# Summing the mixer's coefficients once per four pairs, and a closing product in two passes

## The reference, cut to what matters

```python
xn = layernorm(x)
x = x + gnn(xn) + mix(xn)                 # gnn: attention, 16 heads of 64, mask from 12288 edges
x = x + ffn(layernorm(x))
# mix, per head of 64 columns:
q, k = exp(-square(xn @ Wq + bq) / 2), exp(-square(xn @ Wk + bk) / 2)
coeff = sum(q * k, axis=head columns)     # one number per row and head
mix = (coeff * (xn @ Wv + bv)) @ Wo + bo
# ffn: one of 8 experts is picked (argmin of a loss over the data), then
h = relu(x @ Wd + bd)                     # 64 wide
ffn = (x @ base_W.T + base_b) + (h @ Wu + bu) @ Wc.T + bc
```

## Time and profile before

| What | us |
|---|---|
| median of three runs (476.05, 479.64, 480.69) | 479.64 |
| the profiled execution, its own time | 474.66 |
| its span, first to last instruction | 472.9 |
| PE busy | 465.9 |
| DVE busy | 342.3 |
| ACT busy | 262.2 |
| POOL busy | 157.2 |

### The profile page before, as it was taken

One profiled execution on the slowest core, in us unless ns is written; L12 is line 12 of the kernel. 1 busy time (PEld: TensorE's weight loads), 2 busy tenths in 40 slices (PEclk: granted clock), 3 DMA queues, 4 the chain that ended last, 5 costly groups with the idle time before them and its releaser, 6 DMA issues.

```text
span 472.9 us, 7361 instructions
## 1 busy us (share of the span) xinstructions
PE 465.9 (99%) x2533; PEld 432.4 (91%) x2533; DVE 342.3 (72%) x796; ACT 262.2 (55%) x429; POOL 157.2 (33%) x176
## 2 busy tenths in 40 slices
PE   7999999999999999999999999999999999999996
PEld 5999999999999888999999999999998888888885
DVE  6979966677626259687978888796966794587294
ACT  3734433333324245788989889897974542163170
POOL 3147677777767741002130202212142000050200
PEclk9999999999999999999999999999999999999999
DMA  8877756655444454577675766766679835210463
GB/s 243 325 230 230 239 195 167 176 182 180 154 152 153 133 200 179 175 226 253 205 232 184 235 192 197 247 180 224 192 240 382 308 115 179 89 46 0 155 247 133
DMA packets 39049, 91.92 MB, mean 194 GB/s; under 512 B 7410, under 2 KB 20306, under 8 KB 38884
## 3 DMA queue, kind: packets, MB, share of 16 engines
q1 hardware_dynamic: 33604, 83.15, 54.0%
q0 software_dynamic: 4832, 7.45, 4.7%
q10 hardware_dynamic: 576, 0.85, 0.5%
HBM read 77.96 MB, written 13.47 MB: 193 GB/s over the span
## 4 chain that ended last, share of the span: by engine, by line
PE 87%; DVE 5%; DMA 3%; ACT 3%; issue 1%; SPq 0%; DVEq 0%; ACTq 0%
PE PS L1278 32%; PE PS L1288 28%; PE PS L1283 16%; PE PS L1416 3%; PE PS L1404 2%; DMA turn<-U 2%; PE PS L1535 2%; PE PS L1346 2%; DMA U<-x 1%; DVE U L1076 1%; DVE w_lo L895 1%; PE PS L1266 1%; ACT U L659 1%; PE PS L1539 1%; ACT w_hi L536 1%
## 5 line engine op out<-in xcount | busy, mean ns | idle before, releaser
L895 DVE TENSOR_TENSOR w_lo<-raw,w_hi 128x1024 fp32r<-128x1024 f32 x86 | 104.4, 1225 | 45.0 <-ACT w_hi L536 45.0
L536 ACT ACTIVATE w_hi<-raw 128x1024 fp32r<-128x1024 f32 x87 | 90.8, 1054 | 68.5 <-PE PS L1288 44.1
L454 POOL DMA_INDIRECT table<-evalue,where x96 | 103.0, 1073 | 45.7 <-issue 25.2
L1283 PE MATMUL PS<-xT_hi,w_lo 128*128 128x384 f32 x320 | 61.9, 334 | 0.0
L1278 PE MATMUL PS<-xT_hi,w_hi 128*128 128x384 f32 x320 | 61.9, 334 | 0.0
L1278 PE MATMUL PS<-xT_lo,w_hi 128*128 128x384 f32 x320 | 61.9, 334 | 0.0
L1278 PEld LDWEIGHTS PS<-xT_lo,w_hi 128*128 128x128 f32 x320 | 56.0, 188 | 0.0
L1278 PEld LDWEIGHTS PS<-xT_hi,w_hi 128*128 128x128 f32 x320 | 56.0, 188 | 0.0
L1283 PEld LDWEIGHTS PS<-xT_hi,w_lo 128*128 128x128 f32 x320 | 56.0, 188 | 0.0
L469 POOL TENSOR_TENSOR T_lo<-U,T_hi 128x384 fp32r<-128x384 f32 x8 | 8.2, 1020 | 97.8 <-ACT T_hi L733 97.8
L1288 PE MATMUL PS<-w_hi,T_hi 128*128 128x512 f32 x144 | 40.0, 391 | 0.0
(11 more groups left out here) (241 smaller groups left out, 817.1 us busy)
## 6 DMA issues: line engine op xcount, KB each, us to landing
raw<-weights SPq DMA_DIRECT2D x84, 512.0 KB, 4.6
turn<-U SPq DMA_DIRECT2D x16, 576.0 KB, 4.0
U<-turn SPq DMA_DIRECT2D x64, 144.0 KB, 2.9
U<-key_dram SPq DMA_DIRECT2D x32, 192.0 KB, 4.1
mask<-weights SPq DMA_DIRECT2D x9, 512.0 KB, 5.1
...
```

The source lines that it names most:

```text
L454: pool.indirect_dma_start(tables[g], bass.IndirectOffsetOnAxis(ap=where[:, k:k + 1], axis=0), evalue[:, k:k + 1], None, bounds_check=N * N ...
L536: act.activation(w_hi[slot][:], raw[slot][:], ACT.Copy).then_inc(hi_ready[slot], 1)
L895: dve.tensor_tensor(w_lo[slot][:], raw[slot][:], w_hi[slot][:].bitcast(F32), ALU.subtract).then_inc(lo_ready[slot], 1)
L1283: last = pe.matmul(o, wl, src[0][:, k, :], start=False, stop=(k == KB - 1))
```

## The change

Four edits.

- **Coefficients.** The mixer's columns are permuted on the host so that a group of four pairs (`GROUP`) holds 16 columns (`SHARE`) of each of its eight heads in every pair. The four tiles of exponentials are added up (`feat_sum`), split once, and one pair of matmuls gives the coefficients of all four. The raw values wait in `raw_value(j)`, slices of the attention values that are no longer read, and DVE multiplies four of them after pairs 3 and 7. `mix_hi` and `mix_lo` run four pairs later.
- **x ahead.** POOL issues the fetch of x after `mix_lo(4)`, ahead of the last three, and the fetch of the bias rows after `mix_lo(5)`.
- **Base weights.** The four spare base blocks are loaded and split two blocks later.
- **Close.** Rows 64 to 127 of the P tile hold P again, and `h_main` holds the high part of h over its low part, so one matmul does two passes; `h_side` by `pc[1]` does the third and the side rows (the biases in parts, one row that `h_main` gives up to a row of ones). Row 64's work goes through one row written by ACT. Tile (0, 1) is copied by ACT and added by POOL, DVE adds the other five.

```diff
+def adds(j):
+    return j - j // GROUP
...
@@ -388,19 +414,17 @@
                 load_weights(*slot_use(n + 3), weights[35 + n])
             for b in range(5, 16):
                 load_weights(*C_USES[b], weights[72 + b])
-                if b == 5:
-                    sp.wait_ge(vs_ready, KB)
                 if b == 7:
+                    sp.wait_ge(ml_ready, KB)
                     sp.wait_ge(score_read, KB * 6 + 1)
-                if 5 <= b < 9:
-                    load_weights(*E_USES[(b - 5)], weights[72 + 16 + (b - 5)])
+                if 7 <= b < 11:
+                    load_weights(*E_USES[(b - 7)], weights[72 + 16 + (b - 7)])
             for e in range(4, 8):
                 load_weights(*E_USES[e], weights[72 + 16 + e])
             sp.wait_ge(x2_turned, NT)
...
-            for half in range(2):
+            for half, t, done, count in ((0, 0, y_ready, 1), (0, 2, y_ready, 2), (1, 0, y_ready, 3),
+                                         (0, 1, y_added, 1), (1, 1, y_ready, 4), (1, 2, y_ready, 5)):
                 c = slice(half * HALF, (half + 1) * HALF)
-                for t in range(NT):
-                    sp.wait_ge(y_ready, half * NT + t + 1)
-                    sp.dma_start(out[t * P:(t + 1) * P, c], x_rows[:, t, c]).then_inc(stored, 16)
+                sp.wait_ge(done, count)
...
@@ -488,43 +514,48 @@
                                    ALU.subtract).then_inc(vs_ready, 1)
             for j in range(KB):
-                if j:
+                if j >= GROUP:
                     pool.wait_ge(vs_ready, j)
-                    mix_lo(j - 1)
-                    pool.wait_ge(ml_ready, j)
+                    mix_lo(j - GROUP)
+                    pool.wait_ge(ml_ready, j - GROUP + 1)
                 values(j)
                 if j:
                     pool.wait_ge(vs_ready, j + 1)
                     out_lo(j - 1)
                     pool.wait_ge(ol_ready, j)
-                if j == KB - 1:
+            for j in range(KB - GROUP, KB):
+                mix_lo(j)
+                pool.wait_ge(ml_ready, j + 1)
+                if j == KB - GROUP:
+                    pool.wait_ge(pT_ready, KB * 2 - 1)
+                    pool.wait_ge(block_ready, KB * 6)
+                    pool.wait_ge(feat_ready, KB // GROUP)
+                    pool.dma_start(x_rows, x.rearrange("(t p) d -> p t d", p=P)).then_inc(xr_in, 16)
+                if j == KB - GROUP + 1:
                     pool.wait_ge(ql_ready, KB)
                     pool.dma_start(row_bo, rows[0:2, :].partition_broadcast(P)).then_inc(rows_in, 16)
-            mix_lo(KB - 1)
-            pool.wait_ge(ml_ready, KB)
-            pool.wait_ge(pT_ready, KB * 2 - 1)
-            pool.wait_ge(block_ready, KB * 6)
-            pool.wait_ge(feat_ready, KB)
-            pool.dma_start(x_rows, x.rearrange("(t p) d -> p t d", p=P)).then_inc(xr_in, 16)
             out_lo(KB - 1)
             pool.wait_ge(ol_ready, KB)
...
-            pool.memset(t0l[:, 0:2 * D].bitcast(F32), 0.0).then_inc(aug_zero, 1)
...
+            pool.memset(h_side[R:P, :].bitcast(F32), 0.0).then_inc(side_const, 1)
+            pool.wait_ge(side_const, 1)
+            pool.memset(h_side[R:R + 1, :].bitcast(F32), 1.0).then_inc(side_const, 1)
+            pool.wait_ge(side_const, 2)
+            pool.memset(h_side[side, :].bitcast(F32), 1.0).then_inc(side_const, 1)
+            pool.wait_ge(side_const, 3)
+            pool.memset(pc[1][SIDE_ROW:P, :].bitcast(F32), 0.0).then_inc(pc_zero, 1)
+            pool.wait_ge(pc_zero, 1)
             split_lo(*E_USES[7])
+            pool.wait_ge(hT_hi, 1)
+            pool.tensor_copy(h_side[0:R, :], h_main[0:R, :].bitcast(F32)).then_inc(h_copied, 1)
+            pool.wait_ge(h_low_in, 2)
+            pool.memset(h_main[R:R + 1, :].bitcast(F32), 1.0).then_inc(hT_ready, 1)
+            pool.wait_ge(y_spilt, 1)
+            pool.tensor_tensor(x_rows[:, 1, 0:HALF], spill, x_rows[:, 1, 0:HALF], ALU.add).then_inc(y_added, 1)
...
-                act.activation(sq_q, sq_q, ACT.Exp, scale=-0.5).then_inc(feat_exp, 1)
-                act.wait_ge(feat_exp, j + 1)
-                act.activation(feat[0], sq_q, ACT.Copy).then_inc(feat_hi, 1)
+                if j == 0:
+                    act.wait_ge(vs_ready, 1)
+                if j == GROUP:
+                    act.wait_ge(feat_ready, 1)
+                act.activation(sq_q.rearrange(rows_of_three, t=NT) if j % GROUP else feat_sum,
+                               sq_q.rearrange(rows_of_three, t=NT), ACT.Exp, scale=-0.5).then_inc(feat_exp, 1)
                 split_hi(*ahead[3])
+                if j % GROUP == GROUP - 1:
+                    act.wait_ge(feat_added, adds(j))
+                    act.activation(feat[0].rearrange(rows_of_three, t=NT), feat_sum, ACT.Copy).then_inc(feat_hi, 1)
...
-                act.activation(mix_v, PS[:, 1, 0:N], ACT.Identity,
+                act.wait_ge(vs_ready, j + 1)
+                act.activation(raw_value(j), PS[:, 1, 0:N].rearrange(rows_of_three, t=NT), ACT.Identity,
                                bias=bias[:, 8 * KB + j:8 * KB + j + 1]).then_inc(mixv_ready, 1)
...
-            mix_hi(KB - 1)
+            mix_hi(KB - 4)
+            mix_hi(KB - 3)
             split_hi(*C_USES[2])
             split_hi(*C_USES[3])
             pv_copy(KB - 1, 0)
             turned_hi(KB - 1, 1)
+            mix_hi(KB - 2)
+            mix_hi(KB - 1)
             split_hi(*C_USES[4])
             pv_copy(KB - 1, 1)
             out_hi(KB - 1)
...
-                if 6 <= b < 10:
-                    split_hi(*E_USES[b - 6])
+                if 8 <= b < 12:
+                    split_hi(*E_USES[b - 8])
...
+                act.activation(pc[0][:, c], PS[:, V_BANKS[half], :], ACT.Copy).then_inc(pc_hi, 1)
+                act.wait_ge(bias_ready, 1)
+                act.wait_ge(pc_hi, half + 1)
+                act.activation(pc[1][SIDE_ROW:SIDE_ROW + 1, c], pc[0][0:1, c].bitcast(F32),
+                               ACT.Copy).then_inc(pc_row, 1)
+            act.wait_ge(y_done, 2)
+            act.activation(spill, PS[:, E_BANKS[0][1], :], ACT.Copy).then_inc(y_spilt, 1)
...
-                dve.wait_ge(feat_hi, j + 1)
-                dve.tensor_tensor(feat[1], sq_q, feat[0].bitcast(F32), ALU.subtract).then_inc(feat_ready, 1)
+                if j % GROUP:
+                    dve.wait_ge(feat_exp, j + 1)
+                    if adds(j) > 1:
+                        dve.wait_ge(feat_added, adds(j) - 1)
+                    dve.tensor_tensor(feat_sum, feat_sum, sq_q.rearrange(rows_of_three, t=NT),
+                                      ALU.add).then_inc(feat_added, 1)
                 split_weights(*ahead[3])
+                if j % GROUP == GROUP - 1:
+                    dve.wait_ge(feat_hi, j // GROUP + 1)
+                    high, low = (f.rearrange(rows_of_three, t=NT) for f in feat)
+                    dve.tensor_tensor(low, feat_sum, high.bitcast(F32), ALU.subtract).then_inc(feat_ready, 1)
                 turned_lo(j, 0)
-                dve.wait_ge(coeff_done, j + 1)
-                dve.wait_ge(mixv_ready, j + 2)
-                dve.tensor_tensor(mix_v, PS[:, 0, 0:N], mix_v, ALU.mult).then_inc(mix_ready, 1)
+                if j % GROUP == GROUP - 1:
+                    dve.wait_ge(coeff_done, j // GROUP + 1)
+                    dve.wait_ge(mixv_ready, j + 2)
+                    for i in range(j - GROUP + 1, j + 1):
+                        dve.tensor_tensor(raw_value(i), PS[:, 0, 0:N].rearrange(rows_of_three, t=NT), raw_value(i),
+                                          ALU.mult).then_inc(mix_ready, 1)
...
-            dve.tensor_tensor(hT[1][0:R, :], h_sum[0:R, :], hT[0][0:R, :].bitcast(F32), ALU.subtract).then_inc(hT_ready, 1)
+            dve.tensor_tensor(h_main[R:P, :], h_sum[0:R, :], h_main[0:R, :].bitcast(F32), ALU.subtract).then_inc(h_low_in, 1)
+            dve.wait_ge(side_const, 3)
+            dve.tensor_tensor(h_side[SIDE_ROW:SIDE_ROW + 1, :], h_sum[0:1, :], h_main[0:1, :].bitcast(F32),
+                              ALU.subtract).then_inc(h_low_in, 1)
...
             split_p(0)
+            final_rows(0, 0)
             split_p(1)
-            def final_rows(half):
-                c = slice(half * HALF, (half + 1) * HALF)
-                for t in range(NT):
-                    dve.wait_ge(y_done, half * NT + t + 1)
-                    dve.tensor_tensor(x_rows[:, t, c], PS[:, E_BANKS[half][t], :], x_rows[:, t, c],
-                                      ALU.add).then_inc(y_ready, 1)
-            final_rows(0)
-            final_rows(1)
+            final_rows(0, 2)
+            for t in range(NT):
+                final_rows(1, t)
...
-                pe.wait_ge(feat_hi, j + 1)
+                pe.wait_ge(feat_hi, j // GROUP + 1)
                 pe.matmul(PS[:, 0, 0:N], head_ones[:], feat[0], start=True, stop=False)
-                pe.wait_ge(feat_ready, j + 1)
+                pe.wait_ge(feat_ready, j // GROUP + 1)
```

(46 more changed lines are left out.)

107 lines of the change are left out of this document (63 added, 44 removed).

## The result

Over 21 runs of each, the changed kernel takes 479.06 us in the median and the kernel before 475.19: a ratio of **1.0078 [1.0058, 1.0098]**, 3.7 us slower (two runs of the changed kernel in a slow state, 485.5 and 486.1 us, are not in the ratio). The time lies in the range given, and the change is within 1%, but the sign is wrong: 0.55% of gain was forecast. Part of the closeness is luck: 479.64 was the median of three runs, and 21 runs of the same kernel give 475.19.

What follows compares the result with a forecast made beforehand. PE was taken to bound the pairs without holes, DVE the end. Coefficients -2.08, C block stall +0.2 and close -0.75 gave -2.6 us, carried from the 479.64 median to 477.0; range 473.6 to 480.3.

Steps and rivals of the forecast that it cites:

- the close: Kernel's end: DVE's shorter chain of adds gains 0.75 us; bounds 0.80 gained or 0.3 lost if POOL's add is stretched.
- the chance for slower: Chance of over 1% slower, above 484.4 us: 0.06, from the third rival (4%) and 2% for the unseen.
- the sum: Whole kernel: the terms add to -2.6 us, span 470.3, median 477.0, a gain of 0.55%.
- The C blocks: C block 2: PE stalls 0.2 us for POOL's low part of block 5, bounds 0 and 1.2; block 3 hidden.
- The sum by that rule, 1.2: C block 2: stall of 1.2 us, not 0.2, if VectorE and GpSimd exclude each other for whole instructions.
- The coefficients: Six of eight pairs lose two PE matmuls: 2.08 us less, all on the path; at least 0.
- cost 0: Coefficient work on ACT and DVE costs nothing; bound of 1.4 us per group after pairs 3 and 7.
- my first rival: Grouping returns as waits: DVE's burst twice 1.4 us, or C block 2's tie and stores; 479.6 us, no change; 15%.
- the weight block that the text names: Value job after pair 3's burst: tightest use found, made 280.75 to 281.80, used 283.81, 2.0 us of slack.
- The fetch of x and the base weights: Earlier x fetch and later base blocks: nothing won or lost, 0; bias rows land at 370.8, still covered.
- the slower rival: POOL is held until x's fetch lands, PE resumes near 370: 13 us more, 490; 4%.
- The rival that read the 5 us between them as waits in memory: Timed runs hold waits at x and the C blocks that the profile lacks; half saved gives 474.5; 17%.

Runs made afterwards that it cites:

- e2: Kernel before the change plus a one-column POOL memset waiting for VectorE's sixth and last output tile; 480.81 us, ratio 1.0107.
- e3: Kernel before the change plus a one-column POOL memset waiting for TensorE's first finished output tile; 476.56 us, ratio 1.0028.
- e8: Changed kernel plus one POOL drain after its low part of the last attention output; 502.69 us, ratio 1.0044.
- e9: Changed kernel plus e8's early POOL drain and e7's low parts on VectorE; 496.58 us against 503.58, ratio 0.9877.
- e1: Changed kernel without POOL's late addition and ScalarE's tile copy; VectorE adds six tiles, SyncE stores in order; 474.38 us, ratio 0.998.
- e4: Kernel before the change with only the two-pass closing product, without POOL's addition; 475.46 us, ratio 0.9993.
- e6: e1 with ScalarE's high parts of 6 and 7 earlier and both POOL fetches after low part 6; 474.40 us, ratio 0.9995.
- e7: e6 with low parts 4 to 7 on VectorE and C block 3's split behind the probabilities; 474.33 us, ratio 0.9974.
- e11: Same kernel as e9, measured again; 499.46 us against 496.15 for the kernel before the change.
- e12: Same kernel as e9, measured a third time; 496.85 us against 494.10 for the kernel before the change.
- e5: Kernel before the change with the coefficients, x and base weight edits, old closing product, no late POOL addition; 474.52 us, ratio 0.9996.

## Why the prediction was wrong

**The step that failed is the close.** It said of POOL's add that it "takes 1.4 and ends at 468.3", with "Bounds: 0.80 gained, or 0.3 lost". The add ended at 468.62 and was not stretched (1.28 us, I said 1.4). What the step left out is what an engine does after its last instruction. Giving POOL that add moved POOL's end from 462.1, where its memset ends, to 468.6, and with it the 8.4 us of the drain, past the last store. e2 and e3 show the delay without any of the change, and e8 takes 4.4 us off by one early drain. It could have been read: the drain of 10852 ns stood in the trace of before, ending over 21 us before anybody needed it. None of my rivals had it, and the chance for slower was 0.06.

**The close also earned less than its 0.75 us.** VectorE's chain became shorter by 0.68, where 0.75 was worked out. But of it some 0.35 arrives (61.52 to 61.15 in e9). With POOL's addition in place and its drain settled (e8, e9) the end is no earlier than with six additions on VectorE (e1, e4, e6, e7: 61.14 to 61.21). SP's issue of the last store ended 0.36 us behind VectorE's last addition before (470.31 and 469.95), and 0.65 behind it in the changed kernel (470.18 and 469.53): SP stores (0,1), which comes from POOL, fourth, and two others queue behind it. The text had stores that queue behind POOL's only in its bound of a loss, with a stretched add; the sum had nothing for them.

**The C blocks: the mechanism was right, the size was off.** I took 0.2 us from bounds of 0 and 1.2; the table has 1.00. POOL's last two low parts took 1.90 us each where I counted 1.03, and the second wait was at C block 3, which the text called hidden:

```profile
354.59 0.80 POOL L534 DMA_DIRECT2D U<-x  x1 [0.30 <-POOL T_lo L495]
355.41 1.25 POOL L495 TENSOR_TENSOR T_lo<-V,T_hi 128x384 fp32r<-128x384 f32 x1
...
358.57 3.80 POOL L495 TENSOR_TENSOR T_lo<-V,T_hi 128x384 fp32r<-128x384 f32 x2 [1.03 <-ACT T_hi L776]
```

PE's timeline there shows what came of it. C block 2 starts 1.45 us after its product and C block 3 1.49, where both gaps were 1.07 before, and the first record of block 2 takes 1.66, not 1.55. These three make 0.9 of the 1.0 us:

```profile
356.71 1.66 PE L1361 MATMUL PS<-w_hi,T_hi 128*128 128x512 f32 x6 [0.23 <-POOL T_lo L495]
...
362.42 0.96 PE L1361 MATMUL PS<-w_hi,T_hi 128*128 128x512 f32 x3 [0.26 <-POOL T_lo L495]
```

That VectorE and POOL hold each other up is shown by e6, where the delay moved from one to the other, and e7 (and e9, e11, e12), where it vanished. The rule cited in the prediction (the Trainium skill, SBUF — State Buffer, section "SBUF: two separate sides") has this, and the trace agrees with it: of the four low parts the first, beside no such instruction of VectorE, takes 1.03, the others 1.25, 1.90 and 1.90. The sum by that rule, 1.2, was nearer than mine, in part by luck: it was meant for C block 2 alone, and the loss came at two places, since three of the four low parts met a subtraction of VectorE and not one.

**The coefficients gave 1.4 us of 2.08.** The pairs without them are 20.70 us apart, as foreseen:

```profile
228.73 2.77 PE PS L1351 x16
...
249.43 2.77 PE PS L1351 x16
```

In ten traces with the grouping (the changed kernel, e1, e5 to e12) the pairs take 165.2 us in the mean, in four without it (before, e2 to e4) 166.65. "All on the path" held, "cost 0" on the other engines did not. Most of the missing 0.6 us lies behind the burst of four products, my first rival. VectorE came to pair 4's masks at 270.04, I said 270.0, and at pair 4's keys PE had no wait, as said:

```profile
270.04 0.55 DVE L1116 CUSTOM_DVE_ANT_0 U<-PS,mask 128x384 f32<-128x384 f32 x1
```

But the 1.4 us that pair 4's softmax is late for stay in the order of ScalarE and VectorE, up to the scores of pair 5. ScalarE's copy of the value tile there must be over before PE's last third of the scores. It ended at 288.75 before, ahead of its use, and at 289.38 in the changed kernel, where PE goes on at 289.43. ScalarE in the kernel before:

```profile
286.61 1.17 ACT L647 ACTIVATE probT_hi<-U 128x1152 fp32r<-128x1152 f32 x1
...
288.17 0.58 ACT L718 ACTIVATE U<-PS,bias 128x384 f32<-128x384 f32 x1
```

and ScalarE, then PE, in the changed one:

```profile
287.33 1.17 ACT L678 ACTIVATE probT_hi<-U 128x1152 fp32r<-128x1152 f32 x1 [0.55 <-DMA U<-turn]
...
288.82 0.56 ACT L761 ACTIVATE V<-PS,bias 128x384 f32<-128x384 f32 x1
```

```profile
289.43 0.45 PE L1477 MATMUL PS<-T_hi,q_hi 64*128 64x384 f32 x2
```

From the first scores of pair 5 to those of pair 6 it takes 20.90 to 21.74 us in the ten traces (20.97 in the changed kernel, 21.15 in the mean), where 20.70 was due; pair 4, with the same two matmuls gone, takes 20.70 to 20.73. So the rival came true in small: 0.2 to 1.0 us each time, and the tightest use was not the weight block that the text names (2.0 us of slack). No run moves the burst alone, so this is read from the traces and not tested. Pairs 1 and 6 have such waits in some traces; part of these was there before.

**The fetch of x and the base weights were right, at 0.** The adds now wait for the bias rows, to 370.14, where 370.8 was said; the wait is 3.97 us, where "about 2" was said:

```profile
370.14 3.50 DVE L1192 TENSOR_TENSOR U<-U,Q 128x1024 f32<-128x1024 f32 x3 [3.97 <-DMA Q<-rows]
```

PE has no wait there. POOL held by its fetch, the slower rival, did not happen: the next low part began 0.02 us after the issue ended.

**The level was wrong too.** The sum was laid on the median of three runs; the profiled execution's 474.66 was nearer to what 21 runs gave. The rival that read the 5 us between them as waits in memory explained a difference that 18 more runs did not bear out.
